# One head of an attention phase: a key load, an exponential, a key split and a query split in other places of their queues

## The reference

```
x = x + tanh(g_ffn[0])   * L0_ffn(layernorm(x))            # 8 bit rows times ternary weights
x = x + tanh(g_xattn[1]) * L1_xattn(layernorm(x), ctx, ctx)
x = x + tanh(g_ffn[1])   * L1_ffn(layernorm(x))            # 8 experts of rank 128, top 2
# L1_xattn, for each of the 4 x 8 heads of 128 rows:
qk  = einsum('bdm,bdn->bmn', qh, kh) / sqrt(128)
ret = einsum('bmn,bcn->bcm', softmax(qk), vh)              # kh and vh are both ctx
```

## Time and profile before

| | before |
|---|---|
| median of 3 runs | 1985.94 us |
| lowest and highest run | 1985.0 and 1987.85 us |
| the profiled execution's own time | 1985.46 us |
| its span, first to last instruction | 1983.7 us |
| PE, DVE, ACT, POOL busy | 1851.1, 1559.9, 1264.0, 846.4 us |
| mean granted TensorE clock | 0.986 |

### The profile page before, as it was taken

How to read it: one execution, slowest core, us unless ns; L and a number is a source line. 1 busy time by engine, 2 the same in 40 slices (tenths; PEclk the granted TensorE clock), 3 DMA queues, 4 the chain that set the end, 5 groups by cost and what they waited for, 6 DMA issues and landing times.

```text
span 1983.7 us, 26460 instructions
## 1 busy us (share of the span) xinstructions
PE 1851.1 (93%) x8968; PEld 838.5 (42%) x8968; DVE 1559.9 (79%) x2386; ACT 1264.0 (64%) x2045; POOL 846.4 (43%) x1100
## 2 busy tenths in 40 slices
PE   1699999996699999999999999999999999999998
PEld 0244444442244444444444444444444444444443
DVE  8899999888877777777777777777777777777662
ACT  4798999675656665666665665656656665666650
POOL 3555565333344443444444443443444444444420
PEclk9999999998799999999999999999999999999998
DMA  9587777797888888878888888888888888888772
GB/s 210 160 207 201 225 199 189 190 210 221 159 151 170 169 178 170 168 154 166 170 163 174 165 171 169 170 174 169 160 162 169 164 170 167 165 172 168 152 143 54
DMA packets 923975, 340.50 MB, mean 172 GB/s; under 512 B 849728, under 2 KB 898880, under 8 KB 923840
## 3 DMA queue, kind: packets, MB, share of 16 engines
q1 hardware_dynamic: 923840, 338.81, 80.9%
HBM read 93.36 MB, written 33.55 MB: 64 GB/s over the span
## 4 chain that ended last, share of the span: by engine, by line
PE 73%; issue 4%; DVE 2%; POOL 2%; DMA 1%; ACT 1%; SPq 0%; POOLq 0%; DVEq 0%
PE sc L1080 16%; PE accs L1060 11%; PE accs L1062 11%; PE accs L1061 11%; PE accs L1101 6%; PE accs L1118 6%; PE accs L1102 6%; PE accs L1103 6%; POOL slot L599 1%; DMA slot<-slot 1%; POOL slot L592 1%; PE accs L1129 0%; DMA wb_lo<-in_L_ffn_Wa 0%; DVE tiny L1585 0%; PE accs L1131 0%
## 5 line engine op out<-in xcount | busy, mean ns | idle before, releaser
L1590 DVE SCALAR_TENSOR_TENSOR slot<-arena,tiny,slot 128x1024 f16<-128x1024 f32 x256 | 346.4, 1353 | 169.1 <-ACT slot L885 165.6
L885 ACT ACTIVATE slot<-arena,tiny 128x1024 f16<-128x1024 f32 x256 | 290.9, 1145 | 251.8 <-POOL tiny L710 247.0
L1080 PE MATMUL sc<-arena,slot 128*128 128x512 f16 x1536 | 375.8, 383 | 19.7 <-ACT arena L872 17.3
L708 POOL TENSOR_SCALAR tiny<-tiny 128x1 f32<-128x1 f32 x256 | 117.4, 459 | 519.1 <-ACT arena L872 519.1
L1585 DVE TENSOR_REDUCE tiny<-sc 128x1 f32<-128x1024 f32 x256 | 311.7, 1218 | 20.0 <-PE sc L1080 20.0
L872 ACT ACTIVATE arena<-sc,tiny,head_tab 128x1024 f32<-128x1024 f32 x256 | 308.4, 1205 | 8.6
L1080 PEld LDWEIGHTS sc<-arena,slot 128*128 128x128 f16 x1536 | 147.9, 98 | 211.8 <-ACT arena L872 32.2
L710 POOL TENSOR_TENSOR tiny<-tiny,neg_one 128x1 f32<-128x1 f32 x256 | 224.7, 878 | 21.3
L1101 PE MATMUL accs<-probs,arena 128*128 128x512 f16 x512 | 196.1, 383 | 12.3 <-issue 10.8
L864 ACT ACTIVATE tiny<-tiny,head_tab 128x1 f32<-128x1 f32 x256 | 74.3, 290 | 207.3 <-DVE tiny L1585 207.3
L1060 PE MATMUL accs<-wb_hi,slot 128*128 128x512 f16 x512 | 194.1, 379 | 2.7 <-DMA slot<-slot 2.7
(11 more groups left out here) (214 smaller groups left out, 2907.3 us busy)
## 6 DMA issues: line engine op xcount, KB each, us to landing
arena<-in_x SPq DMA_DIRECT2D x32, 512.0 KB, 4.0
x_scratch<-arena SPq DMA_DIRECT2D x32, 512.0 KB, 3.7
slot<-x_scratch SPq DMA_DIRECT2D x32, 512.0 KB, 3.3
slot<-in_ctx SPq DMA_DIRECT2D x32, 512.0 KB, 4.2
out<-arena SPq DMA_DIRECT2D x31, 512.0 KB, 3.6
slot<-in_L_ffn_Wa SPq DMA_DIRECT2D x12, 512.0 KB, 4.5
slot<-in_L_ffn_Wb SPq DMA_DIRECT2D x9, 512.0 KB, 5.2
wb_hi<-in_ctx SPq DMA_DIRECT2D x64, 64.0 KB, 2.3
```

The costliest lines, as they stand in the source:

```text
L885: act.activation(high, full, ACT.Identity, scale=rinv[c % 4][:]).then_inc(s_ph.sem, 1)
L1080: mm = pe.matmul(sc[:, c % 2, h * HALF:(h + 1) * HALF], q[i][:, c * P:(c + 1) * P], k[j][:, h * HALF:(h + 1) * HALF], start=start, stop=stop)
L1590: dve.scalar_tensor_tensor(out=low, in0=full, scalar=rinv[c % 4][:], in1=high, op0=ALU.mult, op1=ALU.subtract).then_inc(s_pl.sem, 1)
```

## The change

Only iteration n = 1 is changed. On SP, `load_k(2)` stood ahead of the loop; it now stands after `turn_probs(1, 1)`, and `load_k(3)`, which stood after `turn_rows(0)`, stands after `turn_keys(1)`. On ACT, `key_high(2)`, `query_full(2)` and `query_high(2)` stood ahead of `rows_full(0)`; they now stand after `prob_high(1, 2)`, and `exp(1, 2)` stands ahead of `rows_full(0)`. On DVE, `key_low(2)` stands after `prob_low(1, 2)` rather than after `prob_low(1, 0)`, and `row_maxima(1, 2)` stands ahead of `prob_low(1, 1)`.

```diff
-            load_k(2)
             for n in range(1, TILES + 2):
...
+                if n == 1:
+                    load_k(2)
                 if prev:
                     turn_rows(n - 1)
-                if quant:
+                if quant and n > 1:
                     load_k(n + 2)
                 if cur:
                     turn_probs(n, 2)
                     turn_probs(n, 3)
                     turn_keys(n)
+                if n == 1:
+                    load_k(3)
...
                 if cur:
                     exp(n, 0)
-                if nxt:
+                if nxt and n > 1:
                     key_high(n + 1)
                 if cur:
                     prob_high(n, 0)
                     exp(n, 1)
                     prob_high(n, 1)
-                if nxt:
+                if n == 1:
+                    exp(1, 2)
+                if nxt and n > 1:
                     query_full(n + 1)
                     query_high(n + 1)
                 if prev:
                     rows_full(n - 1)
                     rows_high(n - 1)
-                if cur:
+                if n == 1:
+                    exp(1, 3)
+                    prob_high(1, 2)
+                    key_high(2)
+                    query_full(2)
+                    query_high(2)
+                elif cur:
                     exp(n, 2)
                     prob_high(n, 2)
                     exp(n, 3)
+                if cur:
                     prob_high(n, 3)
...
                     prob_low(n, 0)
-                if nxt:
+                if nxt and n > 1:
                     key_low(n + 1)
...
-                if cur:
+                if n == 1:
+                    row_maxima(1, 2)
+                    prob_low(1, 1)
+                elif cur:
                     prob_low(n, 1)
                     row_maxima(n, 2)
...
                     prob_low(n, 2)
+                if n == 1:
+                    key_low(2)
                 if quant:
                     quantise_full(n + 2)
```

## The result

| | before | changed kernel |
|---|---|---|
| median | 1984.56 us (22 runs) | 1987.55 us (22 runs) |
| lowest and highest | 1980.54 and 1988.83 us | 1984.29 and 1992.56 us |
| ratio of times | 1 | 1.0018, 95% interval 1.0011 to 1.0025 |
| the profiled execution: its time, its span | 1985.46, 1983.7 us | 1985.52, 1983.7 us |
| mean granted TensorE clock | 0.986 | 0.988 |

The changed kernel is 0.18% slower, 3.6 us with an interval of 2.2 to 5.0 (the ratio less 1, times 1984.6); the two medians lie 3.0 us apart. The forecast was a delay of 2.6 us. The 0.18% is just inside the 0.2% that was to count as the same, but with 22 runs of each kernel the interval leaves no doubt that the change costs time. The forecast time itself, 1988.5 us, started from a median of 1985.94 over 3 runs. Over 22 runs that median is 1984.56, and 2.6 us on top of it make 1987.2, against 1987.55 measured.

The account below looks back on a forecast made before the run. PE, busy 93% of the span, was taken to set the pace. A gain of 0.2 us up to `scores(1, 6)` and a loss of 2.8 made +2.6 on the 1985.94 median: 1988.5 us, range 1985.0 to 1990.8.

Parts of the forecast that it names:

- Part 1, the key load: SP, head 0: without the load ahead, chunk 7's turn lands sooner and `values(0, 1)` starts 1.85 us earlier.
- the two bounds: SP, chunk 7's turn of head 0: landing time without the load between 4.4 and 5.7 us; 4.4 taken.
- Part 2, exponential 2: ACT, iteration 1: `scores(1, 4)` 5.1 us earlier, `scores(1, 5)` 2.4 earlier; the long wait moves to the latter.
- Part 3, the key and the query: ACT, POOL, DVE: late `query_low(2)` delays `quantise_norm(3)` 3.0 us; `scores(1, 6)` waits 2.2 us, gain gone but 0.2.
- Part 4, what is late next: Head 1's last turns: chunk 7 three microseconds late, slack at most 0.6, so `values(1, 1)` starts 2.4 to 3.0 us later.
- The sum: Whole kernel: -0.2 us up to `scores(1, 6)`, then +2.8, so +2.6 us.
- Absorbed: Rival at head 1's turns: more slack than seen takes up the delay, giving 1985.7 us; chance 0.15.
- The gain is kept: Rival: `query_low(2)` does not hold DVE and POOL; PE keeps 2.4 plus 4.2 us, giving 1979.3; chance 0.05.
- The clock falls once more: Rival: PE's new wait ahead of `scores(1, 6)` brings the 1.2 GHz clock, delay 4.5 us, time 1990.4; chance 0.16.
- Its second way: Same slower case: chunk 7 of head 0 lands no earlier, delay 4.45 us, also 1990.4; within the 0.16.
- The change does not do what it says: Rival on the queues: the steps are not really moved; given no chance.

Follow-up runs that it names:

- e7: The changed kernel run again with no edit: 1987.43 us, ratio 1.0012 to before.
- e1: Changed kernel with `query_full(2)` and `query_high(2)` back directly behind `rows_high(0)`, ahead of `exp(1, 3)`: 1983.56 us, ratio 0.9999 to before.
- e3: Changed kernel with `query_low(2)` on POOL done twice, same result: 1989.96 us, ratio 1.0028 to before.
- e4: Kernel before with only `exp(1, 2)` ahead of `rows_full(0)` and `row_maxima(1, 2)` ahead of `prob_low(1, 1)`: 1985.41 us, ratio 1.0004.
- e5: Kernel before with `load_k(2)` behind `turn_probs(0, 7)`, `key_high(2)`, `exp(1, 2)` behind `prob_high(1, 1)`, query before `exp(1, 3)`, `key_low(2)` behind `prob_low(1, 1)`: 1984.73 us, ratio 1.0000.
- e6: Kernel before with only `load_k(3)` moved, from behind `turn_rows(0)` to behind `turn_keys(1)`: 1984.41 us, ratio 0.9996.
- e8: Kernel before with `load_k(2)` behind `turn_probs(0, 7)`, `key_high(2)` behind `prob_high(1, 1)`, `key_low(2)` behind `row_maxima(1, 2)`: 1982.76 us, ratio 0.9988.
- e10: Second run of e5, the kernel before with load, key, exponential and query steps all placed: 1982.34 us, ratio 0.9985.
- e2: Changed kernel with `load_k(2)` back ahead of the loop on SP: 1988.22 us, ratio 1.0019 to before.

## Why the prediction was right, point by point

The forecast was made in times of one trace, so it is best held against two. Here are its marks less 514.35, where `scores(1, 0)` had started before, beside what came (us from the start of `scores(1, 0)`):

| | forecast | changed kernel | e7 |
|---|---|---|---|
| `scores(1, 4)` | 16.15 | 17.47 | 16.08 |
| `scores(1, 5)` | 22.55 | 23.72 | 22.33 |
| norm | 29.25 | 30.50 | 29.43 |
| `scores(1, 6)` | 34.15 | 35.41 | 34.35 |
| `values(1, 1)` | about 58.6 | 59.49 | 58.52 |

e7 meets every mark within 0.25 us. In the first profile the times below agree within 0.6 us in part by luck: `scores(1, 0)` started 0.76 us earlier than before, and the wait of 1.12 us behind it took that back and a little more.

**Part 1, the key load.** Right. The wait ahead of `values(0, 1)` is gone, and the turn of chunk 7, issued at 516.5, took 1.83 us to issue and landed after 4.4, the shorter of the two bounds. In e7 `values(0, 1)` starts 6.18 us behind `scores(1, 0)` where it was 8.05 before: 1.87 us earlier, against a forecast of 1.85. The two turns of chunks 6 and 7 in the changed kernel, which answer to the earlier trace rows:

```profile
L503 SPq DMA_TRANSPOSE probs<-slot x2: 1830/2058/2285, 514.1 to 516.5; - x2
...
DMA to landing us min/median/max: 4.4/4.4/4.5
```

One detail was not: the load was to cost `turn_rows(0)` nothing. SP's rows in the changed kernel show that the turn behind the load (L510) now takes 3.51 us to issue:

```profile
533.80 0.57 SPq L458 DMA_DIRECT2D slot<-in_ctx  x1
534.54 3.51 SPq L510 DMA_TRANSPOSE slot<-slot  x1
```

In e7 it took 3.70, and PE waited 0.46 us for it ahead of the router (0.36 in e1, 0.15 in e3). The load does to the turn behind it here what it had done to chunk 7's before; it is only less dear.

**Part 2, exponential 2.** Right in place and size: `scores(1, 4)` was forecast for 530.5 and came at 531.06, `scores(1, 5)` for 536.9 and came at 537.31. That the long wait would only move one chunk on, and the clock fall all the same, e4 shows alone. The wait was to be some 5 us and was 3.73 (4.20 in e7), and the clock fell a chunk sooner than said: `scores(1, 4)`, behind a wait of 1.97 us, already took 2.52 us, and the stretch up to `scores(1, 5)` was granted 0.53. What PE lost by that came out of the wait that followed. The clock of the changed kernel, as windows (columns as the earlier trace rows):

```profile
531.00:537.30 6.30, 2.52 (x6) 0.67 (x6) 3.55 (x3) 3.81 (x7) 0.80 (x2) 0.53 0.94 208
537.30:545.50 8.20, 8.05 (x43) 3.34 (x44) 3.86 (x4) 4.32 (x4) 3.56 (x3) 0.74 0.67 130
545.50:556.00 10.50, 7.92 (x38) 3.42 (x36) 9.96 (x22) 6.69 (x10) 3.83 (x9) 1.00 0.60 106
```

**Part 3, the key and the query.** Right, and this is the whole of the loss. `quantise_norm(3)` was forecast for 543.6 with 3 us of idle DVE ahead of it, and came at 544.09 with 3.28; `scores(1, 6)` was forecast for 548.5 with a wait of 2.2, and came at 549.00 with 2.58. In e7 that wait was only 0.83 us, and the start the same to 0.2 us of the forecast: PE came later, since its clock stayed low until 548.7 us and the router waited 0.46, and the exponential set the start either way. `query_low(2)` took 2.13 us, as assumed. e1 undoes this part alone and the slowdown is gone; e3 doubles its last step and the slowdown grows.

The 2.13 held because DVE stood still. Where DVE had begun a step of two inputs 0.09 to 0.15 us ahead of it, the same instruction took 3.11 to 3.17 us (before, e1, e5, e6, e8 to e10); with DVE at rest it took 2.12 or 2.13 (the changed kernel, e2, e3, e7). In e4 it began first and took 2.12, and DVE's step was the one held, for 1.89 us in the place of 1.23. The Trainium skill, "SBUF — State Buffer", section "Who interferes with whom", has GpSimd and VectorE exclude each other in that case; by that rule the traces agree.

**Part 4, what is late next.** Right: `values(1, 1)` was forecast for about 573 and came at 573.08, behind a new wait of 2.32 us that before did not have. Chunk 7's turn was issued at 568.4, 3.0 us later than the 565.4 of before. The half that was wrong: I had also put a wait of 1 to 2 us ahead of `output(0, 0)`; it does not wait. That cost nothing in the sum, since it was counted as the first share of the same delay.

**The size.** The sum was +2.6 us. Over A the second run of the same kernel shows +2.56, the first +3.53, of which 1.12 is the chance wait. The ratios give +3.6 (2.2 to 5.0) and, in e7, +2.4 (0.6 to 4.4); the medians 3.0 and 2.3. Its last line was loosely built: it adds the 0.2 us that PE wins at `scores(1, 6)` to the delay, though PE waits again at `values(1, 1)` and so keeps nothing of it, and it takes the same 0.2 off the 3.0 once more. What the queues do is what part 4 says: the norm's delay less the slack at `values(1, 1)`, 3.0 less 0.6 at the least, which gives 2.4 to 3.0. Measured in e7: the norm 3.14 us later, the slack 0.58 (29.67 less 29.09), together 2.56. That the sum hit this to a few hundredths is luck, since the first profile less its wait gives 2.4; that it lay between 2.4 and 3.0 is not. That the single span of the changed kernel equals that of before is no evidence against: behind iteration 1 PE meets a dozen small waits ahead of `values`, whose sum differs from run to run (from 560 us on 9.0 us in 14 before, 10.4 in 13 after, 6.2 in 11 in e8), and head 0 shifts too.

**The rivals.** *Absorbed*: false, the slack at `values(1, 1)` was 0.58 us, as small as the rows had shown. *The gain is kept*: false, but e1, e5 and e10 show what it needs, the query ahead of `exp(1, 3)`; even then A is only 1.0 to 2.5 us under before, of the 6.6, because the long wait ahead of `scores(1, 5)` stays, and e8 has as much by its load alone. *The clock falls once more*: false for the changed kernel, since the clock was back at full before the new wait and stayed there behind it (the third window; `scores(1, 6)` takes 1.47 us). e3 shows that it was a real rival: with a wait of 4.57 us it does fall, while behind 3.02 us in e2 it did not. Its second way, that chunk 7 of head 0 lands no earlier, is false too: it landed after 4.4 us. *The change does not do what it says*: false.

## What to carry to other kernels

When a step is moved back in a queue to let an urgent one pass, look not at who needs its result for the product, but at who must wait before writing to its buffer: here `quantise_norm` of the next-but-one tile waited for the low part of a query, done at 543.98 us, that `scores(2, 0)` needed only at 561.96. A wait on the critical engine that is fed by one chain of another engine's steps moved on by one chunk when the order within that chain was changed (e4); what did shorten the stretch here was work taken off a queue ahead of the chain (the load ahead of chunk 7's turn, e8). Where a gain of 2 us stands against a scatter of 8, measure a stretch between two marks of the trace in several executions and let the medians confirm it.

## What the runs showed of the hardware that was not expected

- **Head 0 shifts by microseconds with nothing changed.** The same changed kernel started `scores(1, 0)` at 513.59 us in one execution and at 518.46 in the other. In the second, PE came out of a wait at the lower clock: its `values(0, 0)` begins with matmuls of 0.59 to 0.63 us instead of 0.38. That makes up 1.45 of the 4.87 us. The other 3.42 lie ahead of `values(0, 0)`, and their cause is not shown.

```profile
511.84 0.59 PE L1113 MATMUL accs<-probs,arena 128*128 128x512 f16 x1 [1.41 <-DMA probs<-slot]
```

- **Of two steps that collide, the one that starts later stands still until the other is through.** `query_low(2)` alone takes 2.12 or 2.13 us, and DVE's steps of two inputs take 1.23 to 1.28. Wherever such a step of DVE started while `query_low(2)` ran, it ended 1.08 us behind the end of `query_low(2)`: `prob_low(1, 2)` in 2.94 us before, having started early, and in 1.53 in e1, having started late; `rows_low(0)` in 1.89 in e4. `query_low(2)` itself was stretched by 1.0 us only where `output_low(4)` had started ahead of it on DVE, and then ended 2.0 us behind that step. So one such meeting can cost both engines: before, `query_low(2)` lost 1.0 us and `prob_low(1, 2)` 1.7. The row of before, and the two of e4, where POOL was first:

```profile
537.77 2.94 DVE L1590 SCALAR_TENSOR_TENSOR slot<-arena,tiny,slot 128x1024 f16<-128x1024 f32 x1
...
538.27 1.89 DVE L1615 TENSOR_TENSOR slot<-slot 128x1024 f16<-128x1024 f32 x1 [2.70 <-ACT slot L914]
...
536.96 2.12 POOL L683 TENSOR_TENSOR slot<-slot 128x1024 f16<-128x1024 f32 x1
```

- **A load ahead of a turn costs more in the turn's issue than in its own.** The key load of 512 KB took 0.57 to 0.75 us to issue where it stood directly ahead of a turn. The turn behind it paid more: chunk 7's of head 0 took 3.62 to 3.67 us to issue behind the load (before, e2, e4, e6) and 1.77 to 2.21 without it, `turn_rows(0)` 3.31 to 3.70 behind the load (the changed kernel, e1, e3, e7) and 1.32 without it. A load is not the only thing that does this: chunk 6's turn of head 1 took 3.75 us behind `turn_hidden(0)`.
